# A two-layer graph attention kernel on one core: the second layer's batches written out, and the first layer's first scores of a strip moved ahead of the last values

## The reference

```
h = max(layernorm(x), 0);  x = x + L0(h, adj, ...)
h = max(layernorm(x), 0);  x = x + L1(h, adj, ...)

L0:  q, k, v = h @ W.T + b, in 4 heads of 64
     scores = clip(q k / 8, -10, 10), per chunk of 256 nodes; -10 where adj is 0
     attn = softmax within each chunk; ctx = sum over the 8 chunks of attn @ v
     out = layernorm(ctx @ Wo.T + bo + h) * gamma + beta
L1:  q = h @ W, in 4 heads;  e = leaky_relu(q.a_src (row) + q.a_dst (column), 0.2)
     e = -9e15 where adj is 0;  out = elu(softmax(e) @ q)
```

## Time and profile before

| what | value |
|---|---|
| median of three runs | 5075.81 us |
| the profiled execution | 5075.05 us |
| its span, first to last instruction | 5073.2 us |
| instructions | 139595 |
| layer 0's stretch (chunk steps) | about 106 to 3480 us |
| layer 1's steps | 3503 us to the end |
| mean granted TensorE clock | 0.98 of full speed |

### The profile page before, as it was taken

The page is one execution under the profiler, slowest core; times in us unless marked ns, Lnnn a source line. Parts: engine busy times, 40 slices in busy tenths (PEclk is TensorE's granted clock), DMA queues, the critical chain, the costliest instruction groups (busy, mean ns, idle before and its releaser), DMA issues. The chain is left out here.

```text
span 5073.2 us, 139595 instructions
## 1 busy us (share of the span) xinstructions
PE 4789.6 (94%) x56352; PEld 4391.7 (87%) x56352; DVE 3717.4 (73%) x7020; ACT 2999.6 (59%) x3377; POOL 1446.4 (29%) x1694
## 2 busy tenths in 40 slices
PE   6999999999999999999999999985998989989898
PEld 4998899889898899888988889974988988989898
DVE  6676667666676666666667666655988888989898
ACT  4444444444444444444444444436988988989897
POOL 3343344334344344433434334331010000000100
PEclk9999999999999999999999999997999999999999
DMA  5000100010001000010000000004122121121211
GB/s 207 18 18 18 30 26 18 22 26 26 22 18 26 18 22 26 18 31 18 26 22 19 25 18 22 14 13 122 30 74 67 35 74 47 53 72 41 63 63 36
DMA packets 116657, 195.79 MB, mean 39 GB/s; under 512 B 7552, under 2 KB 91904, under 8 KB 113792
## 3 DMA queue, kind: packets, MB, share of 16 engines
q1 hardware_dynamic: 100960, 142.71, 8.6%
q0 software_dynamic: 15008, 43.53, 3.5%
HBM read 110.43 MB, written 38.03 MB: 29 GB/s over the span
## 5 line engine op out<-in xcount | busy, mean ns | idle before, releaser
L577 PEld LDWEIGHTS outs<-v_s,probs 128*128 128x128 f32 x16384 | 1978.6, 192 | 111.6 <-issue 27.6
L690 ACT ACTIVATE slot<-slot,shift 128x1024 f32<-128x1024 f32 x1024 | 1111.6, 1088 | 1590.0 <-PE slot L567 1590.0
L577 PE MATMUL outs<-v_s,probs 128*128 128x128 f32 x16384 | 1993.1, 275 | 5.0 <-DVE ctx_part L847 5.0
L831 DVE SCALAR_TENSOR_TENSOR probs<-slot,bound 128x1024 f32<-128x1024 f32 x1024 | 1251.2, 1224 | 708.4 <-ACT slot L690 707.7
L1416 ACT ACTIVATE cond<-s_all,d_sign 128x1024 bf16<-128x1024 f32 x1024 | 1122.3, 1139 | 138.7 <-DVE u L1581 133.4
L393 POOL TENSOR_TENSOR ctx_sum<-ctx_sum,ctx_part 128x256 f32<-128x256 f32 x896 | 650.4, 731 | 1017.1 <-DVE ctx_part L847 1016.7
L566 PE MATMUL slot<-q_hl,k_hl 128*128 128x512 f32 x2048 | 895.0, 437 | 42.4 <-DVE probs L831 24.2
L1581 DVE TENSOR_TENSOR u<-cond,mask 128x1024 f16<-128x1024 bf16 x1024 | 695.4, 689 | 187.3 <-PE sums L1305 103.5
L567 PE MATMUL slot<-q_hl,k_hl 128*128 128x512 f32 x2048 | 804.3, 393 | 0.0
L1301 PE MATMUL sums<-x_mixed,u 128*128 128x130 f16 x8192 | 804.0, 222 | 0.0
L1305 PE MATMUL sums<-x_mixed,mask 128*128 128x65 f16 x8192 | 776.0, 195 | 17.1 <-issue 17.1
(11 more groups left out here) (144 smaller groups left out, 3782.9 us busy)
## 6 DMA issues: line engine op xcount, KB each, us to landing
q_hl<-q_hl POOLq DMA_DIRECT2D x128, 256.0 KB, 3.7
s_all<-s_turned SPq DMA_DIRECT2D x64, 512.0 KB, 4.0
xs<-in_x SPq DMA_DIRECT2D x32, 512.0 KB, 4.4
x<-y SPq DMA_DIRECT2D x32, 512.0 KB, 3.1
o_s<-x SPq DMA_DIRECT2D x16, 1024.0 KB, 5.5
out<-o_s SPq DMA_DIRECT2D x16, 1024.0 KB, 5.9
x_s<-x SPq DMA_DIRECT2D x28, 512.0 KB, 5.3
probs<-in_adj SPq DMA_DIRECT2D x11, 1024.0 KB, 5.2
```

The source lines that it names most:

```text
L577: end = nc.tensor.matmul(outs[i % OUTS][:, q, :], probs[:, i % PROBS, r, q * P:(q + 1) * P], v_s[:, c * JC + r, h * E1:h * E1 + P], start= ...
L690: nc.scalar.activation(slot[:, :, :], slot[:, :, :], ACT.Exp, bias=shift[:, 0:1], scale=SCALE).then_inc(act_done, 1)
L831: nc.vector.scalar_tensor_tensor(probs[:, i % PROBS, :, :], spot(kind, "step", s, i)[:, :, :], P_LOW, bound[:, (i // H) % 2, :, :], ALU.ma ...
```

## The change

In layer 0, at every strip boundary within a batch (s = 0 to 2), TensorE's `scores` of step 0 of the next strip is issued at i = 33, ahead of `values` of step 31, instead of after it. Slots, semaphores and the other engines' programs stay as they are. In layer 1 the loops over batches on TensorE, ScalarE and VectorE are written out, so that the batch number is a constant everywhere; the order of work is the same. SP's and POOL's loops stay, and so do all loops of layer 0.

```diff
@@ layer 0, TensorE, batch()
-                        if i < STEPS:
+                        if i < STEPS and not (i == 0 and s > 0):
                             scores(s, i)
+                        if i == STEPS + LAG - 1 and s < NS - 1:
+                            scores(s + 1, 0)
                         if i in t_pairs(s) and not last:
@@ layer 1, TensorE
-            with pe.Fori(0, B - 1) as b:
+            for b in range(B - 1):
                 batch(b, False)
             batch(B - 1, True)
@@ layer 1, ScalarE (and the same three lines on VectorE)
             batch(0, 0, True, False)
-            with act.Fori(0, (B - 2) // 2) as n:
-                for odd in (1, 0):
-                    batch(n * 2 + 2 - odd, odd, False, False)
+            for b in range(1, B - 1):
+                batch(b, b % 2, False, False)
             batch(B - 1, 1, False, True)
```

More of the change, by code:

```diff
@@ L1732, in _ @@
             batch(0, 0, True, False)
-            with dve.Fori(0, (B - 2) // 2) as n:
-                for odd in (1, 0):
-                    batch(n * 2 + 2 - odd, odd, False, False)
+            for b in range(1, B - 1):
+                batch(b, b % 2, False, False)
             batch(B - 1, 1, False, True)
```

## The result

The changed kernel took 4998.71 us in the median of four runs (4994.66 to 5003.94), the kernel before 5078.98 us in four. The ratio is 0.985, with a 95% interval of 0.9833 to 0.9867: 80 us less. In layer 1, lines are shifted by 2 on TensorE, POOL and ScalarE (L1296 is L1298, L1228 is L1230) and by 1 on VectorE (L1581 is L1582).

A forecast was written before the change was run, and what follows sets the result against it. TensorE, busy in 94% of the span, was taken to bound the kernel, so only its standstills could give time back. 5075.05 - 62.85 - 13.14 - 2.4 = 4996.7, forecast as 4997 us, range 4985 to 5016.

The forecast's parts named there:

- the moved scores: Layer 0's strip boundaries: two TensorE stalls of 1.04 us together become one ahead of the turn, gaining 2.4 us in all.
- The edges: Layer 1, six TensorE back edges: straight code makes each boundary stretch like the loop's exit, 24.67 us; 62.85 us gained.
- Unit m=1: Layer 1, after each boundary: POOL's mean_neg no longer held, units take 22.49 instead of 25.12 us; 13.14 us gained.
- the gap: Layer 1: VectorE standing idle ahead of pick 15 (0.91 us in batch 4) tells that mean_neg in m=1 is not held.
- The query copy's margin: Layer 0's strip boundaries: copied queries land 0.3 us ahead of TensorE's arrival at scores 0, so cost zero.
- (a): Layer 1: mean_neg stays held, each boundary's m=1 at 25.12 us; total 5012 us; chance 0.22.
- (b): Layer 0's strip boundaries give most of their 1.04 us as the turn's 3.85 us shrinks; down to 4975 us; chance 0.08.
- (c): Layer 1: the unrolling brings nothing, the wait is not the jump's; 5073 us; chance 0.03.
- (d): Layer 0: the moved scores find the query copy late, 24 times; slower, 5109 us; chance 0.03.

The follow-up runs named there:

- e5: The changed kernel with TensorE's layer-1 loop put back over pairs of batches, two back edges instead of six: 5000.83 us, ratio 0.9907.
- e4: The kernel before with only ScalarE's and VectorE's layer-1 loops written out, TensorE's kept: 5047.36 us, ratio 1.0004.
- e3: The kernel before with only TensorE's layer-1 loop written out, ScalarE's and VectorE's kept: 4996.35 us, ratio 0.9899.
- e8: The changed kernel with layer 0's loops written out too, on all five engines: 4996.4 us, ratio 0.9827.
- e10: The changed kernel with three small POOL fills ahead of each mean_neg and POOL's layer-1 loop written out: 4992.15 us, ratio 0.9824.
- b1: The kernel before, unchanged, run again for a trace in the third group: ratio 0.9997 to itself.
- e1: The kernel before with only layer 0's moved scores, layer 1's loops kept: 5038.0 against 5046.58 us, ratio 0.9983.
- e9: The changed kernel with no loop left in either layer and mean_neg made on ScalarE: 4963.6 us, ratio 0.9769.
- e6: The changed kernel with mean_neg made on ScalarE instead of POOL: 4978.29 us, ratio 0.986.

## Why the prediction was right, and where it was not

The sum, 78.4 us, met 72.7 in the profiled executions and 80 in the medians; the terms met less well. That the total came within 2 us in the medians is in part luck: the moved scores gave 10 us more than forecast, and holds at m=3, which the prediction gave no term, took 7 back.

**The edges** (62.85 forecast, 60.95 measured) are shown, step by step: the wait is the jump's (e5), TensorE's comes last (e4), VectorE's lay under it (e3), and the loop's exit was the right measure for straight code. Taking the price from stretches of equal work rather than from the 50.1 us of waits brought the miss from 10.9 down to 1.9 us. The exit was one sample, though. The same stretch from batch 6 to 7 took 23.1 to 24.7 us in the other traces, so with another draw the term could have come out up to 9 us larger.

**Unit m=1** (13.14 forecast, 13.6 measured) was right in amount, and in the changed kernel's trace by its own reason: all six units had the gap, 0.66 to 1.26 us, and none was held. As a rule the reason is too strong. With the gap 3 of 16 were held in the five traces, without it 2 of 14 were not. Nor does straight code always give the gap: three of six units in e8 and three of six in e10 had none. So the term as written held because the gap stood at all six boundaries and because this comparison ran where holds occur. With mean_neg as it was, 10 of 12 units m=1 behind a back edge were held there (before, b1), and 1 of 12 behind a straight boundary (the changed kernel, e8). By what path the gap acts, 5.5 us ahead of mean_neg, was not found. On the chip of e1 to e4 the term was zero, and the unrolling gained 56 us, not 76. Three holds at m=3 instead of one took 7.3 us back; the prediction had left these out. What a hold costs is read from e8 against e9, with POOL out of the chain: 2.2 us at m=1 and 3.1 to 4.1 at m=3. That VectorE is what holds mean_neg is argued from where every hold of 4.5 us ends, 0.15 us after den begins; no run changed VectorE's instructions. The Trainium skill (SBUF — State Buffer, Who interferes with whom) has the right kind of pair. By its rule the one that issues first has the shared port for its whole instruction; read as a wait of one VectorE instruction (0.69 us for a pick), that is too short for the 4.49 and 4.58 us of these rows.

**The moved scores** (2.4 forecast, 12.3 measured): the mechanism was as written, two stalls traded for one ahead of the turn. The term was mis-sized in the step from the turn to scores 2. It took 0.85 us, not the turn's busy 1.09 or a little less. The turn came 3.73 us after values 31, not 3.85: it follows POOL's last add by 0.13 in both orders, but the add ended 3.60 instead of 3.72 us after values 31 began. In the old order values 31 began from a standstill, and its second matmul came 0.21 us after its first instead of 0.11. And scores 0 followed values 30 by 1.70, not 1.80. These three, 0.4 us at 24 places, are the 10 us that were missed. The query copy's margin held: scores 0 waited for it by at most 0.1 us at any of the 24 places. Most take the usual 15.8 to 16.1 us; one took 16.54, where the second copy of that boundary took 4.8 us to land (at 1132.54) and scores 2 stood 0.21 us for it.

**The rivals.** (a) did not happen at m=1; holds came at m=3 instead and took half of its 15 us. (b) happened to a half: 0.51 of 1.04 us per boundary, 0.12 of it by its own path, the add that ends earlier. The range's lower end was to take in "a third of (b)'s surplus"; from 4997 down to 4985 is over half of the 22 us down to 4975, so the range was wider than its words. (c) and (d) did not happen.

## What to carry to other kernels

Price a loop's back edge by comparing its stretch with the loop's exit, and write out the slowest engine's loop first: here it gave 50 of 56 us. The loops of engines close behind it then show, at 3 to 4 us per jump here. When a move trades a stall for another, size the rest from start to start of neighbours, not from busy times, since pipelined groups overlap (here by 0.1 to 0.25 us) and that was most of this gain. Look at tiny POOL operations in chains beside a busy VectorE: half a microsecond of work (0.47 us) cost its unit 2 to 4 us when held, and making it on ScalarE cost nothing that the runs could tell (e6). One trace of one chip doesn't show whether such a term exists: it was 13 us in the first comparison and zero in two groups.

## What the runs showed of the hardware that was not expected

The same kernel took 5047 and 5085 us on different chips, and the holds make most of it: layer 1 with its loops took 1529.0 us in e1 and 1567.8 in b1, and 36 of these 39 us lie in units m=1 to m=4. No mean_neg over 0.47 us stands in the seven traces of the first two groups that have it on POOL, and in the other five 3 to 9 of about 28 take 4.5 us. With the start 0.1 us later and fills ahead (e10) they stood at m=1 and m=2 and none at m=3. Some held units also ran at a lower granted clock: 25.0 and 25.1 us (m=1) and 28.6 and 28.7 (m=3) go with 0.93 and 0.94, 24.6 (m=1) and 27.6 (m=3) with 1.00. The back-edge stretches had 0.81 to 0.90 against 0.93. A boundary's jump cost 7 to 12 us in layer 1. In layer 0, where TensorE runs about 22,500 matmuls in 3400 us instead of 33,500 in 1570, a batch boundary with loops cost 0 to 4 us.
